# Building looked-up weights on TensorE: a four-buffer hand-off checked once per four planes instead of once per plane

## The reference

```python
def _ghost_linear(x, idx, lut):
    w = lut[idx]                       # idx: 0..15, lut: 16 values
    return jnp.einsum('bsh,oh->bso', x, w)
...
xn = _layernorm(x, axis=-1)            # x: (2, 4096, 2048)
# attention: Q, K = relu(xn W + b) * decay, V = xn W + b, 16 heads of 128
#   out = (Q (K^T V)) / (Q sum(K)); out Wo + bo
gate = _ghost_linear(xn, lut, gate_idx)   # 2048 -> 5504
up   = _ghost_linear(xn, lut, up_idx)     # 2048 -> 5504
h = silu(gate) * up
ffn = _ghost_linear(h, lut, down_idx)     # 5504 -> 2048
out = x + attention + ffn
```

## Time and profile before

| | us |
|---|---|
| three runs | 4957.17, 5073.18, 5076.64 (median 5073.18) |
| the profiled execution, its own time | 4834.9 |
| its span on the slowest core | 4833.4 |
| spans of the eight cores | 4801.5 to 4833.4 |
| PE busy / DVE busy / ACT busy / POOL busy in that span | 3572.3 / 3004.5 / 522.7 / 414.7 |

### The profile page before, as it was taken

The page is one execution under the profiler, slowest core; times in us unless marked ns, Lnnn a source line. Parts: engine busy times, 40 slices in busy tenths (PEclk is TensorE's granted clock), DMA queues, the critical chain, the costliest instruction groups (busy, mean ns, idle before and its releaser), DMA issues. The chain is left out here.

```text
span 4833.4 us, 45872 instructions; the slowest of 8 cores (4801.5 to 4833.4 us)
## 1 busy us (share of the span) xinstructions
PE 3572.3 (74%) x16399; PEld 1552.8 (32%) x16705; DVE 3004.5 (62%) x3433; ACT 522.7 (11%) x715; POOL 414.7 (9%) x428
## 2 busy tenths in 40 slices
PE   0588888888885625888777755959987888856665
PEld 0233333333332212333333322424333333322222
DVE  0588886888855623766777754748758888850000
ACT  4222222222220011000000000010000000000000
POOL 0000000000001100111111110101100000000000
PEclk9999999999996867999888877989999999979989
DMA  7211111111102132101000112121122222202222
GB/s 245 90 46 46 46 46 40 48 47 46 48 7 72 53 107 70 35 33 40 33 33 33 37 55 68 37 88 40 38 85 87 81 75 84 82 34 78 79 78 75
DMA packets 91161, 297.99 MB, mean 62 GB/s; under 512 B 11639, under 2 KB 33655, under 8 KB 79673
## 3 DMA queue, kind: packets, MB, share of 16 engines
q1 hardware_dynamic: 59484, 185.19, 11.4%
q0 software_dynamic: 31456, 109.86, 6.5%
HBM read 218.98 MB, written 76.02 MB: 61 GB/s over the span
## 5 line engine op out<-in xcount | busy, mean ns | idle before, releaser
L222 PE MATMUL ps_acc<-plane,eye_sb 128*128 128x512 bf16 x4947 | 1182.1, 400 | 176.7 <-DVE plane L205 171.5
L205 DVE TENSOR_SCALAR plane<-gb,lutb 128x2048 bf16<-128x2048 bf16 x1264 | 1004.2, 819 | 263.0 <-PE ps_acc L222 183.5
L162 DVE TENSOR_TENSOR wt<-wt,plane 128x2048 bf16<-128x2048 bf16 x750 | 918.7, 1225 | 57.9 <-issue 2.6
L222 PEld LDWEIGHTS ps_acc<-plane,eye_sb 128*128 128x128 bf16 x5056 | 509.7, 102 | 840.3 <-issue 313.9
L159 DVE TENSOR_SCALAR plane<-gb,lutb 128x2048 bf16<-128x2048 bf16 x750 | 560.1, 747 | 0.0
L507 PE MATMUL ps_rot<-wk_bf,xnT_sb 128*128 128x512 bf16 x1985 | 514.3, 418 | 60.1 <-ACT xnT_sb L471 55.2
L519 PE MATMUL ps_rot<-wv_bf,xnT_sb 128*128 128x512 bf16 x2015 | 457.1, 379 | 5.0 <-issue 4.9
L1105 PE MATMUL ps<-arena 128*128 128x512 bf16 x1349 | 322.7, 381 | 94.9 <-DMA arena<-w2h 93.5
L1119 DVE TENSOR_TENSOR xo<-ps,xo 128x512 f32<-128x512 f32 x32 | 22.1, 692 | 502.5 <-PE ps L1105 438.2
L211 DVE CAST wt<-ps_acc 128x2048 bf16<-128x2048 f32 x79 | 181.0, 2291 | 218.8 <-PE ps_acc L222 218.8
L507 PEld LDWEIGHTS ps_rot<-wk_bf,xnT_sb 128*128 128x128 bf16 x2048 | 206.6, 106 | 335.4 <-issue 163.9
(11 more groups left out here) (92 smaller groups left out, 1794.6 us busy)
## 6 DMA issues: line engine op xcount, KB each, us to landing
xt<-xb SPq DMA_DIRECT2D x32, 1024.0 KB, 4.8
gi<-g POOLq DMA_DIRECT2D x86, 256.0 KB, 3.8
w0h<-wt POOLq DMA_DIRECT2D x43, 512.0 KB, 3.0
w1h<-wt POOLq DMA_DIRECT2D x43, 512.0 KB, 3.0
w2h<-wt POOLq DMA_DIRECT2D x43, 512.0 KB, 3.0
arena<-w2h SPq DMA_DIRECT2D x172, 128.0 KB
xt<-wkT SPq DMA_DIRECT2D x16, 1024.0 KB, 5.6
xt<-wvT SPq DMA_DIRECT2D x16, 1024.0 KB, 5.5
```

The costliest lines, as they stand in the source:

```text
L162: vector.tensor_tensor(wt[:], wt[:], planes[v % 2][:], ALU.add)
L205: i = vector.tensor_scalar(planes[v % 4][:], gb[:], float(v), lutb[:, v : v + 1], ALU.is_equal, ALU.mult)
L222: i = tensor.matmul(ps_acc[:, j4 * 512 : (j4 + 1) * 512], eye_sb[:], planes[v % 4][:, j4 * 512 : (j4 + 1) * 512], start=(v == 0), stop=(v ...
```

## The change

DVE checks for free buffers once in four planes, before plane 0, 4, 8 and 12 of a tile, and then waits until *all* planes before this one have been consumed (`s_pm >= p`, where it was `p - 3`). PE checks for planes once in four, and then waits until all four of the group have been written (`+ 4`, where it was `+ 1`). The number of plane buffers stays at four, the instructions that do the work stay the same, and so do the semaphore increments. Per tile, 12 of 16 waits go on either side.

```diff
@@ g_vec_a (DVE)
             for v in range(16):
                 p = a * 16 + v
-                if p >= 4:
-                    vector.wait_ge(s_pm, p - 3)
+                if v % 4 == 0 and p >= 4:
+                    vector.wait_ge(s_pm, p)
                 i = vector.tensor_scalar(planes[v % 4][:], gb[:], float(v),
                                          lutb[:, v : v + 1], ALU.is_equal, ALU.mult)
                 inc(i, "s_pl", s_pl, 1)
@@ g_pe (PE)
             for v in range(16):
-                tensor.wait_ge(s_pl, a * 16 + v + 1)
+                if v % 4 == 0:
+                    tensor.wait_ge(s_pl, a * 16 + v + 4)
                 if v == 0:
                     tensor.wait_ge(s_gv, k)
                 for j4 in range(4):
```

## The result

The change made the kernel slower by 23%. The median of nine runs is 6090.53 us (5938.93 to 6136.89), against 4965.94 us (4835.21 to 5076.64) for ten of the kernel before.

The account below looks back on a forecast made before the run. PE was taken as the bound in a running tile, DVE right behind. 4835 us before, plus 918 without the clock and 253 for the clock, gave 6006; plus 119 for the median, 6125 us. Range 5880 to 6420.

Parts of the forecast that it names:

- The turn: Between groups of four planes in a weight tile, PE gets nothing for 3.24 us, three times a tile: 768 us.
- The first group: At each weight tile's start PE waits for four planes instead of one: 75 + 85 + 14 us.
- The 85: First planes of 25 back-to-back tiles, where POOL's cast falls into the planes: 3.4 us more each, 85 us.
- What is hidden: Growth of two weight tiles vanishes in PE's 45 us wait for the second half of the output weights: 24 us off.
- What is removed: 24 waits a tile go; upper bound of a gain 114 us in all, taken as nothing.
- The clock: PE's clock falls in every second new gap at 1.69 us, 214 us, plus 39 us at other tile starts: 253 us.
- falls in every gap: Rival: PE's clock falls in all 253 new gaps, 467 us of clock, 6220 us before the median allowance; chance 0.20.
- holds: Rival: PE's clock falls in none of the 253 new gaps, 5753 us before the median allowance; chance 0.12.
- The frame: Allowance from profiled execution to median of runs: half of the median's distance, 119 us.
- each hand-off puts its latency on the path: Rival: the 12 removed hand-offs a tile cost 0.24 us each, so 228 us are gained, 4607 us; chance 0.01.
- the marks that I named: Signs expected in the profile after: run lengths, plane-group times, engine idle times, the shrunken load wait, unchanged stages, granted clock.

Follow-up runs that it names:

- the look-ahead: Kernel before with per-plane checks, DVE writing the next weight tile's first three planes before copying the present one out of PSUM: ratio 0.9757 to the kernel before.

## Why the prediction was right

The time fell inside the range (5880 to 6420; 6125 forecast, 6090.5 measured), and the growth of the profiled execution was 1104 us against 918 + 253 = 1171. Two misses offset each other in the total: the sum of the parts was 67 us too high, and the allowance for the median 33 us too low. Step by step:

- **The turn.** Right in mechanism, 2 to 3% too dear. I had 3.24 us; it is 3.00 us of idle time and 0.16 of drain, 3.16. The term mis-sized is DVE to PE, 0.24 us by the start of a plane in the earlier trace rows less its 0.75 us; measured behind four planes it is 0.15. 237 turns are 749 us where I had 768.
- **The first group.** PE's idle time for planes grew by 1064.1 - 171.5 = 893 us. 237 x 3.00 = 711 of it are turns, so 182 lie at first groups; I had 75 + 85 + 14 = 174. The 85 was the one too small: I took off up to 1.04 us a tile for a second wait that the kernel before pays already, and by its timeline only one tile had it. 25 x 3.9 = 97 closes most of the distance. In B5a the wait behind the 34 matmuls is 0.98 us, I had 1.0.
- **What is hidden.** The wait for the second half of the weights went from 45 to 13.5 us, where I said about 20. PE's waits ahead of the output projection's matmuls for weights fell together from 132.6 to 101.3 us, 31 us where I had 24:

```profile
L912 PE MATMUL ps_w<-arena 128*128 128x512 bf16 x503 | 116.5, 389 | 101.8 <-ACT arena L896 101.3
```

- **What is removed.** Nothing shows as a gain. Four planes in a row took 2.73 us with a met wait before each and take 2.74 with one wait. Eight buffers with the same few waits are still slower than the kernel before, by the first group.
- **The clock.** I took a fall in every second gap at 1.69 us. By the timeline it was 82 of 237, at 163 / 82 = 2.0 us each: 163 us where I had 0.5 x 1.69 x 231 = 195. At the first groups 63 runs took 348 us instead of 63 x 3.61 = 227, which is 120 us, of which the kernel before already paid 84 (its 79 tiles took 1187 us instead of 79 x 13.97 = 1104); net 36, and I had 58 (39 and, for B2, 19). This is the term that was most off, 199 us where I had 253, and the main reason that the sum came out high. "Every second" was a choice between bounds and no reading, and that a share too high met a price too low is luck. The reason that I gave for more falls than in B2 before, that PE has worked for only 3.5 us ahead of the gap, isn't borne out: the share is 35%, and in B2 of the kernel before 4 of the 11 tiles behind 3.1 to 3.3 us of idle time were slowed (I read 3 of 10). That the clock fell in some gaps and held in others was the likeliest case, and so it went; the cases "falls in every gap" (6220 in this frame) and "holds" (5753) both miss the profiled 5939. Why it falls in one gap and not in the next is open.
- **The frame.** I added 119 us for the distance between a profiled execution and the median; it was 6090.5 - 5938.9 = 152.

The sum by what was measured: 893 idle, 237 x 0.16 = 38 drain, 163 + 36 clock, less 31 hidden, is 1099, and the time ahead of B1 and behind B5a adds 9 - 4 = 5; the profiled executions differ by 1104. The drain is in the 3.16 us of a turn, so it isn't a further cause. The rival "each hand-off puts its latency on the path", by which the change would gain, fell by the sign. A hand-over stands on the path where the engines take turns (the 0.34 us a turn above); in the running tile of the earlier trace rows it doesn't.

Of the marks that I named, the runs of 16 matmuls at about 3.5 us (3.61), the groups of four planes in 2.7 and the nearly unchanged rest came as said. Two did not. DVE's idle time ahead of its planes is 1273 us, where 183.5 + 79 x 3 x 3.6 = 1037 was forecast: it is 3.87 us behind an undisturbed group, and longer behind the slowed ones, the first groups above all, which that figure left out. The granted clock was to be near 0.7 to 0.8 if half the gaps brought a fall; it is 0.78 in B1, 0.83 in B2 and B3 together (0.85 before) and 0.82 in B5a (0.87 before). A mean over time hides the falls, since idle gaps at the upper level count too.

## What to carry to other kernels

When waits are made coarser, count the buffers against the new unit: a hand-off checked in units of n needs 2n buffers, and a wait that lets the producer fill one unit while the other is in use (four buffers in pairs were wholly in turns with the wait at `p`, and overlapped at `p - 2`). Without both the two engines take turns, and then the producer's whole writing time, here 0.68 us a plane, stands in the consumer's path. Price such a change by the producer's work per turn, not by the number of waits saved: in two running engines the waits that were met cost nothing here, and seven turns of two planes took the same time as three of four. An engine that sits in front of a copy and waits for the last results is the place for the next tile's first pieces, as the look-ahead's 2.4% shows.

## What was not expected of the hardware

- The clock in a regular pattern of bursts and gaps isn't settled by the length of a gap: of 237 groups behind the same idle time of 3.0 us 155 kept the upper level and 82 didn't. The share differs by place: 47 of 79 behind a tile's first group, 35 of 158 behind its second and third. With gaps of 1.67 us between groups of 1.9 us none of the slowed groups had a fall that began in such a gap; in 47 cases one from before outlasted it.
- A slowed burst doesn't tell by itself that the gap before it was the cause. The granted clock of the stretch has to be read, from where it fell; it also showed a third level, 0.81, on four cores of one run.
- Matmuls with zero weights and zero data held the clock up: with 12 of them in each gap none of 237 groups was slowed.
